# Attention stage of a hybrid block: scores first, and the weighting between the two maxima

## The chip, the cores and the metric

One core of one Trainium2 chip runs the whole program. The metric is the device time in microseconds (us); the kernel before has a median of 874.27 us over three runs (874.11 to 877.36).

## What is computed

The input is 16 sequences of 256 rows of 128 numbers. The block runs a long convolution (S4D), a mixture of 8 experts with the two best per row, an attention with 16 heads of 8 numbers, and the mixture again:

```python
x = x + _L0_attn_a_ref(_layernorm(x, axis=-1), ...)
x = x + _L0_ffn_ref(_layernorm(x, axis=-1), ...)
x = x + _L0_attn_b_ref(_layernorm(x, axis=-1), L0_attn_b_Wqkv, L0_attn_b_Wout)
x = x + _L0_ffn_ref(_layernorm(x, axis=-1), ...)
```

The change lies in the attention, of which this is the core:

```python
logits = jnp.einsum('bihd,bjhd->bhij', q, k) * scale
logits = logits + SLOPES[None, :, None, None] * rel[None, None, :, :]
logits = jnp.where(causal[None, None, :, :], logits, -jnp.inf)
attn = jax.nn.softmax(logits, axis=-1)
out = jnp.einsum('bhij,bjhd->bihd', attn, v).reshape(Bc, Tc, Dc)
return out @ Wout
```

## The kernel before

`attention_stage` (line 1730) handles one sequence (a batch, b) after another, 16 in all, and each in 4 quarters of 4 heads (G = 0 to 3); quarter x is 4b + G, so there are 64. The softmax needs the largest logit of each row before the exponential. It is found by a first set of score matmuls, rows of queries against keys, whose result VectorE reduces; the row maxima then travel through two transposes and a small DMA into two rows of the operand QPAD, so that the second set of score matmuls (keys against queries) yields logits with the maximum already subtracted.

Every engine runs a program written out by hand, in order, and meets the others at semaphores. On TensorE (`quarter_of`, line 2056) a quarter has these blocks:

- `maxima(y, 0)` and `maxima(y, 1)` (lines 1956 to 1973): the first set, four masking matmuls (L1953) and four score matmuls (L1970) on half-height (64 row) tiles of the array. Tile 0 gives 512 numbers per partition, tile 1 gives 1024. Both write banks 2 and 3, so each waits (`m_red`) until VectorE's reduction (L2226) of the other has read them. They run 4 and 5 quarters ahead.
- `scores(x)` (L1947, L1994, L1998): the second set, also on 64 row tiles, into banks 5 to 7. It waits (`exps`) until ScalarE has read the quarter before. In quarters 0 and 2 it also waits for the DMA of the row maxima (`mrow_in`, L1859).
- `weigh(x - 1)` (L2027, L2028): probabilities times values, f32, on tiles of 128 rows by 32 columns, into half of bank 4. It waits for the exponential of its quarter and, in every second quarter, until ScalarE's `take_out` (L2152) has emptied bank 4 (`ot_set`).
- transposes and projections on the whole array: G = 0 `turn_out` (L2045) and `project` (L1933), G = 1 `project_out` (L2053) and `values` (L1941), G = 2 and 3 `turn_maxima` (L1978) and `turn_back` (L2039). In a few batches G = 3 also has the gate or the ranks of the expert choice (`route.gate`, `route.rank`).

ScalarE's order in a quarter: in G = 1 `take_out` of the batch before, in G = 2 `values` and the normalised rows of an earlier batch (`batches.scalar`, L1134), in G = 3 `take_out` of this batch; then `expo` (L2148) on banks 5 to 7; then `out_high` (L2157) and `highs` (L2133) in G = 0 and `maxima_rows` (L2143) in G = 2 and 3. VectorE: the reduction of tile 0, one or two small operations, the reduction of tile 1, further small ones (`split`, L2218, in G = 1 behind the first reduction). SyncE's queue per batch: load of the spread queries and keys (L1849, L1852), their store (L1842, six DMAs, once `split` is done), the row maxima of both halves (L1859, two DMAs each), the transposes for the next stage (L1143). GpSimd takes each finished batch (row statistics of L2248): norm scalars (L1111 to L1121), rows (L1126, L1127), and for 16 of the tiles the sending to the expert lists (L1058, L1071).

Of the kernel before, what the change touches and what calls it, by code (L numbers as in the profile page):

```python
# [1729 lines left out]
def attention_stage(nc, t):  # L1730
# [13 lines left out]
    with ExitStack() as ctx:  # L1744
# [50 lines left out]
        def after(eng, s, n):  # L1795

            if n > 0:
                eng.wait_ge(s, n)
# [6 lines left out]
        def batch(c):  # L1805
            return 0 <= c < NB

        def quarter(x):
            return 0 <= x < LAST

        def gate_group(b):

            return (b - 7) // 4 if b >= 7 and (b - 7) % 4 == 0 and (b - 7) // 4 < ROUTED_IN_ATTENTION else None

        def rank_group(b):

            early = gate_group(b - 2)
            return early if early is not None and early < SENT_IN_ATTENTION else last_rank(b)
# [104 lines left out]
        def _(pe):  # L1923
# [20 lines left out]
            def mask_later(out, a, half, start):  # L1944

                first = HALF * (a + 1 - half)
                pe.matmul(out[:, :, HALF * half:HALF * half + HALF], LATER_ROWS[PAIR[a], first:first + P],  # L1947
                          LATER[PAIR[a], :, HALF * a:HALF * a + HALF], start=start, stop=False, skip_group_check=True)
# [7 lines left out]
            def maxima(y, tile):  # L1956

                c, G = divmod(y, HG)
                if G == 0 and tile == 1:
                    pe.wait_ge(qk_in[c % 3], 48 * (c // 3 + 1))  # L1960
                after(pe, m_red, 2 * y + 1 - tile)
                keys, queries = P * tile + P, slice(P * tile, P * tile + P)
                out = [ps[2 + a][:, 0:2 * keys].rearrange("p (s n) -> p s n", n=keys) for a in range(2)]
                for a in range(2):
                    mask_earlier(out[a][:, :, P * tile:P * tile + P], a, 0, True)
                for a in range(2):
                    mask_earlier(out[a][:, :, P * tile:P * tile + P], a, 1, False)
                for s in range(2):
                    for a in range(2):
                        ins = pe.matmul(out[a][:, s], QPAD[c % 3][PAIR[a], s, G, queries], KST[c % 3][PAIR[a], G, 0:keys],  # L1970
                                        start=False, stop=True, skip_group_check=True)
                        if s == 1:
                            ins.then_inc(m_mm, 1)

            def turn_maxima(c, h):
                pe.wait_ge(m16, 2 * c + h + 1)
                for tile in range(TPB):
                    ins = pe.transpose(ps[0].bitcast(F16)[0:16, P * tile:P * tile + P],  # L1978
                                       M16[:, h, tile].rearrange("p s a i -> p (s a i)"), ID16)
                ins.then_inc(mt_mm, 1)  # L1980

            def scores(x):

                c, G = divmod(x, HG)
                if G % 2 == 0:
                    pe.wait_ge(mrow_in[G // 2], 32 * (c + 1))
                if x == 0:
                    pe.wait_ge(middle.low, 4)
                after(pe, exps, x)
                early = [ps[5 + a].rearrange("p (h t n) -> p h t n", t=TPB, n=P)[:, :, 0] for a in range(2)]  # L1990
                late = [ps[7][:, SEQ * a:SEQ * a + SEQ].rearrange("p (h n) -> p h n", n=P) for a in range(2)]

                def early_scores(a):
                    return pe.matmul(ps[5 + a], KST[c % 3][PAIR[a], G, 0:P], QPAD[c % 3][PAIR[a], :, G, :], start=False,  # L1994
                                     stop=True, skip_group_check=True)

                def late_scores(a):
                    return pe.matmul(ps[7][:, SEQ * a:SEQ * a + SEQ], KST[c % 3][PAIR[a], G, P:2 * P],  # L1998
                                     QPAD[c % 3][PAIR[a], :, G, P:2 * P], start=False, stop=True, skip_group_check=True)
                mask_later(late[0], 0, 0, True)  # L2000
                mask_later(early[1], 1, 0, True)
                mask_later(late[0], 0, 1, False)
                mask_later(early[1], 1, 1, False)
                late_scores(0).then_inc(st_mm, 1)
                early_scores(1)
                mask_later(early[0], 0, 0, True)
                mask_later(early[0], 0, 1, False)
                pe.wait_ge(st_mm, 3 * x + 1)
                mask_later(late[1], 1, 0, True)
                mask_later(late[1], 1, 1, False)  # L2010
                early_scores(0).then_inc(st_mm, 1)
                late_scores(1).then_inc(st_mm, 1)

            def weigh(x):

                c, G = divmod(x, HG)
                pe.wait_ge(exps, x + 1)
                if G == 0:
                    pe.wait_ge(vset, c + 1)
                if G % 2 == 0:  # L2020
                    after(pe, ot_set, 2 * c + G // 2)
                half = ps[4][:, SEQ * (G % 2):SEQ * (G % 2) + SEQ]
                for g in range(GH):
                    out = half[32 * g:32 * g + 32, :]
                    early = PR[G % 2][:, g // 2, SEQ * (g % 2):SEQ * (g % 2) + SEQ]
                    late = PR[G % 2][:, 2, P * g:P * g + P]
                    pe.matmul(out, V32[c % 2][:, 0, 4 * G + g, :], early, start=True, stop=False)  # L2027
                    ins = pe.matmul(out[:, P:2 * P], V32[c % 2][:, 1, 4 * G + g, :], late, start=False, stop=True)  # L2028
                ins.then_inc(av_mm, 1)
# [12 lines left out]
            def turn_out(c):  # L2042
                pe.wait_ge(att, 2 * c + 2)
                for tile in range(TPB):
                    ins = pe.transpose(ps[1][:, P * tile:P * tile + P], ATT[:, tile, :], t.ID)  # L2045
                ins.then_inc(fa_mm, 1)
# [8 lines left out]

            def quarter_of(b, G):
                x = HG * b + G
                if quarter(x + 4):
                    maxima(x + 4, 0)
                if quarter(x):  # L2060
                    scores(x)
                if G == 3:
                    if gate_group(b) is not None:
                        for c in range(4 * gate_group(b), 4 * gate_group(b) + 4):
                            batches.landed(pe, c)
                        after(pe, mrow_set, min(2 * b + 3, 2 * NB))
                        route.gate(pe, gate_group(b), ps[0])
                    if rank_group(b) is not None:
                        after(pe, mrow_set, min(2 * b + 3, 2 * NB))
                        route.rank(pe, rank_group(b), ps[0])  # L2070
                if quarter(x + 5):
                    maxima(x + 5, 1)
                if G == 0:
                    if batch(b - 2):
                        turn_out(b - 2)
                    if batch(b + 3):
                        project(b + 3)
                if G == 1 and batch(b - 2):
                    project_out(b - 2)
                if G == 2:  # L2080
                    if batch(b + 1):
                        pe.wait_ge(vset, b + 2)
                        turn_maxima(b + 1, 0)
                    if batch(b - 1):
                        turn_back(b - 1, 0)
                if G == 3:
                    if batch(b + 1):
                        after(pe, mrow_set, 2 * b + 3)
                        if gate_group(b) is not None:
                            route.logits_taken(pe, gate_group(b))  # L2090
                        if rank_group(b) is not None:
                            route.ranks_taken(pe, rank_group(b))
                        turn_maxima(b + 1, 1)
                    if batch(b - 1):
                        turn_back(b - 1, 1)
                if b == -1 and G == 0:
                    middle.turn(pe, 2)
                    middle.turn(pe, 3)
                if b == 0:
                    middle.turn(pe, 4 + G)  # L2100
                if quarter(x - 1):
                    weigh(x - 1)
                if G == 1 and batch(b + 1):
                    values(b + 1)

# [370 lines left out]
```

## Time and profile before

| what | value |
|---|---|
| median of three runs | 874.27 us (874.11 to 877.36) |
| time of the profiled execution | 877.4 us, of which the span of the trace is 875.6 us |
| TensorE busy over the span | 618.8 us (71%) |
| VectorE busy | 622.3 us (71%) |
| ScalarE busy | 443.5 us (51%) |
| GpSimd busy | 458.8 us (52%) |
| first and last exponential of the attention | start at 415.3 and 628.2 us |

The span is the time between the first and the last instruction of one execution. Matmuls are pipelined, so the time of one in a row is its passage, not what the next one waits; the distance between the starts of two blocks is what a block costs. PE is TensorE's matmul side, PEld its weight loads, DVE VectorE, ACT ScalarE, POOL GpSimd, SPq the queue of SyncE.

### The profile page before, as it was taken

What the parts mean: (1) busy time and instruction counts of PE and PEld (TensorE: products, weight loads), DVE (VectorE), ACT (ScalarE), POOL (GpSimd) and SP (SyncE); (2) the same over time, 40 slices, a digit from 0 to 9 for tenths busy, and PEclk for the clock granted to TensorE, in tenths of its full rate; (3) what the DMA queues carried; (4) which work ended last, traced back from release to release, by engine and by line L of the source; (5) the groups of instructions that cost most, each with busy time, mean ns of one, the idle gap of its engine ahead of it and who ended that gap; (6) DMA issues with size and microseconds to landing.
All of it is one profiled execution on the core that took longest, in us unless ns stands there. A gap on an engine that the chain in (4) does not pass through costs nothing. (4 is left out here: it accounts for less than half of the span.)

```text
span 875.6 us, 21952 instructions
## 1 busy us (share of the span) xinstructions
PE 618.8 (71%) x7826; PEld 454.7 (52%) x7826; DVE 622.3 (71%) x1397; ACT 443.5 (51%) x873; POOL 458.8 (52%) x591
## 2 busy tenths in 40 slices
PE   0569975780089999125899999999714884999950
PEld 0354433560069999113556666655502563999940
DVE  6997887682078888387778888888513872888856
ACT  5634456760045556162767666666603332555534
POOL 1238758887557777410003223565765880677760
PEclk9968987995579999755899999999956996999985
DMA  9510002341044554332123233241110412444518
GB/s 287 144 38 1 0 8 70 71 90 50 32 83 90 94 94 89 132 116 70 57 64 90 67 88 87 80 119 52 42 34 28 83 34 48 85 100 96 100 28 283
DMA packets 131850, 70.51 MB, mean 81 GB/s; under 512 B 89535, under 2 KB 118725, under 8 KB 131746
## 3 DMA queue, kind: packets, MB, share of 16 engines
q1 hardware_dynamic: 121042, 50.46, 23.9%
q0 software_dynamic: 9088, 16.88, 6.8%
q10 hardware_dynamic: 1616, 1.77, 0.7%
q8 instruction: 67, 1.10, 0.5%
q14 instruction: 37, 0.30, 0.1%
HBM read 26.61 MB, written 30.50 MB: 65 GB/s over the span
## 5 line engine op out<-in xcount | busy, mean ns | idle before, releaser
L1500 ACT ACTIVATE ARENA<-banks,ARENA 128x256 f32<-128x256 f32 x312 | 122.3, 476 | 98.7 <-PE banks L1460 94.4
L2226 DVE TENSOR_REDUCE ARENA<-banks 128x4 f32<-128x1024 f32 (+1 forms) x128 | 122.8, 959 | 39.2 <-PE banks L1970 37.7
L1458 PE MATMUL banks<-ARENA,W1H 128*128 128x256 f16 x312 | 88.1, 282 | 62.3 <-DMA ARENA<-slots 61.5
L2148 ACT ACTIVATE ARENA<-banks 128x1536 f32<-128x1536 f32 x64 | 92.7, 1448 | 38.2 <-PE banks L1994 38.2
L1472 PE MATMUL banks<-W2L,ARENA 128*128 x624 | 110.0, 219 | 2.3 <-DVE ARENA L1513 2.3
L1474 PE MATMUL banks<-W2H,ARENA 128*128 x624 | 109.7, 219 | 0.0
L1473 PE MATMUL banks<-W2H,ARENA 128*128 x624 | 109.7, 219 | 0.0
L1448 POOL DMA_INDIRECT expert_out_g<-ARENA x78 | 77.8, 997 | 48.8 <-issue 26.2
L1448 POOL DMA_INDIRECT expert_out_f<-ARENA x78 | 81.4, 1043 | 33.1 <-issue 23.5
L1532 DVE TENSOR_TENSOR ARENA<-ARENA 128x1024 f16<-128x1024 f32 x78 | 95.6, 1225 | 2.7
L1058 POOL DMA_INDIRECT slots<-ARENA,PLACE x64 | 77.4, 1210 | 26.0 <-issue 17.5
L1459 PE MATMUL banks<-ARENA,W1H 128*128 128x256 f16 x312 | 88.0, 282 | 0.0
L1460 PE MATMUL banks<-ARENA,W1L 128*128 128x256 f16 x312 | 87.9, 282 | 0.0
L1071 POOL DMA_INDIRECT slots<-ARENA,PLACE x64 | 77.3, 1208 | 19.1 <-issue 14.6
L1530 DVE CAST ARENA<-ARENA 128x1024 f16<-128x1024 f32 x78 | 55.0, 706 | 35.0 <-ACT ARENA L1500 34.7
L1458 PEld LDWEIGHTS banks<-ARENA,W1H 128*128 x312 | 31.5, 101 | 67.6 <-issue 63.6
L1472 PEld LDWEIGHTS banks<-W2L,ARENA 128*128 128x128 f16 x624 | 61.0, 98 | 4.1 <-issue 2.9
L1473 PEld LDWEIGHTS banks<-W2H,ARENA 128*128 128x128 f16 x624 | 61.0, 98 | 1.6
L1474 PEld LDWEIGHTS banks<-W2H,ARENA 128*128 128x128 f16 x624 | 61.0, 98 | 0.0
L1953 PE MATMUL banks<-ARENA 64*128 64x128 bf16 x512 | 37.9, 228 | 29.3 <-DVE ARENA L2226 16.9
L488 PE MATMUL banks<-XN,ARENA 128*128 128x512 f32 x64 | 33.7, 688 | 34.2 <-ACT XN L395 29.8
L1518 DVE COPY ARENA<-B 128x4 f32 x78 | 17.8, 282 | 45.9 <-issue 45.9
(324 smaller groups left out, 1773.2 us busy)
## 6 DMA issues: line engine op xcount, KB each, us to landing
spread<-ARENA SPq DMA_DIRECT2D x96, 64.0 KB
ARENA<-expert_out_f SPq DMA_DIRECT2D x8, 512.0 KB, 7.6
ARENA<-spread SPq DMA_DIRECT2D x16, 256.0 KB, 3.0
ARENA<-spread SPq DMA_DIRECT2D x32, 128.0 KB, 2.8
ARENA<-expert_out_g SPq DMA_DIRECT2D x8, 512.0 KB, 7.3
XT<-in_w SPq DMA_DIRECT2D x10, 256.0 KB, 7.7
slots<-EMPTY SPq DMA_DIRECT2D x16, 129.0 KB, 4.3
ARENA<-in_w SPq DMA_DIRECT2D x8, 256.0 KB, 6.6
```

What stands on the lines that cost most here:

```text
L1058: nc.gpsimd.indirect_dma_start(xs, bass.IndirectOffsetOnAxis(ap=t.PLACE[:, 0, i:i + 1], axis=0), ROWI[:, i, :], None).then_inc(sent[i % GR ...
L1448: nc.gpsimd.indirect_dma_start(yo, bass.IndirectOffsetOnAxis(ap=target, axis=0), Y[i % 4][:, h], None, bounds_check=2 * NT * P - 1, oob_is ...
L1458: pe.matmul(out, t.W1H[:, e, ms], XST[i][:, 0], start=True, stop=False)
L1459: pe.matmul(out, t.W1H[:, e, ms], XST[i][:, 1], start=False, stop=False)
L1460: ins = pe.matmul(out, t.W1L[:, e, ms], XST[i][:, 0], start=False, stop=True)
L1472: pe.matmul(out, hh, t.W2L[:, e, m, :], start=(m == 0), stop=False)
L1473: pe.matmul(out, hh, t.W2H[:, e, m, :], start=False, stop=False)
L1474: ins = pe.matmul(out, hl, t.W2H[:, e, m, :], start=False, stop=(m == MT - 1))
L1500: ins = nc.scalar.activation(HF[i % 2][:, m], UP[i % 2][:, m], ACT.Gelu, bias=BIAS[i % 4][:, m:m + 1], scale=1.0 / WS)
L1532: dve.tensor_tensor(H16[i % 4][:, 1], HF[i % 2], H16[i % 4][:, 0], ALU.subtract).then_inc(split, 1)
L2148: nc.scalar.activation(PR[x % 2], t.psum_all[:, 5:8, :], ACT.Exp, scale=1.0 / LOGIT).then_inc(exps, 1)
L2226: dve.tensor_reduce(MX[:, G // 2, tile, :, :, G % 2].rearrange("p s a -> p a s"), src, AX.X, ALU.max).then_inc(m_red, 1)
```

## The change

Only TensorE's `quarter_of` is altered. `scores(x)` comes ahead of `maxima(x + 4, 0)`, and `weigh(x - 1)` moves from behind the transposes and projections to directly behind `maxima(x + 4, 0)`, ahead of the gate or ranks and of `maxima(x + 5, 1)`. No instruction is added or removed, no buffer and no semaphore changes, and the other engines' programs stay as they are.

```diff
             def quarter_of(b, G):
                 x = HG * b + G
+                if quarter(x):
+                    scores(x)
                 if quarter(x + 4):
                     maxima(x + 4, 0)
-                if quarter(x):
-                    scores(x)
+                if quarter(x - 1):
+                    weigh(x - 1)
                 if G == 3:
                     if gate_group(b) is not None:
...
                 if b == 0:
                     middle.turn(pe, 4 + G)
-                if quarter(x - 1):
-                    weigh(x - 1)
                 if G == 1 and batch(b + 1):
                     values(b + 1)
```

## Rows read from the trace of the kernel before

**Rows 1.** Page, granted TensorE clock in 40 slices of the span, tenths of full speed.

```profile
PEclk9968987995579999755899999999956996999985
```

**Rows 2.** Waits between 440 and 600 us: who waited for whom; total us, times, longest.

```profile
ACT ARENA L2148 <- PE banks L1994: 30.5, 38, 2.1
...
PEld banks L1953 <- DVE ARENA L2226: 17.9, 58, 0.4
```

**Rows 3.** Timeline, TensorE, batch 2, G = 0: start us, us, engine, line, count [idle before].

```profile
444.50 0.29 PE L1953 MATMUL banks<-ARENA 64*128 64x128 bf16 x4
...
444.74 0.28 PE L1947 MATMUL banks<-ARENA 64*128 64x128 bf16 x4
...
445.30 0.27 PE L1998 MATMUL banks<-ARENA 64*128 64x256 f16 x1
...
445.72 0.11 PEld L1953 LDWEIGHTS banks<-ARENA 64*128 64x128 bf16 x4 [0.38 <-DVE ARENA L2226]
...
446.15 0.44 PE L2045 MATMUL banks<-ID,ARENA 128*128 128x128 f32 x2
...
446.32 0.21 PEld L1933 LDWEIGHTS banks<-XT,QKWH 128*128 128x128 f16 x2
...
446.98 0.27 PE L1933 MATMUL banks<-XT,QKWL 128*128 128x256 f16 x1
...
447.18 0.66 PE L2027 MATMUL banks<-ARENA 128*32 128x256 f32 x8
...
447.99 0.28 PE L1953 MATMUL banks<-ARENA 64*128 64x128 bf16 x4
```

**Rows 4.** Timeline, VectorE, the two reductions of the same quarter.

```profile
444.97 0.69 DVE L2226 TENSOR_REDUCE ARENA<-banks 128x4 f32<-128x512 f32 x1 [0.24 <-PE banks L1970]
...
446.29 1.23 DVE L2226 TENSOR_REDUCE ARENA<-banks 128x4 f32<-128x1024 f32 x1 [0.63 <-PE banks L1970]
```

**Rows 5.** Timeline, ScalarE, batch 2, and the first exponential of batch 3.

```profile
445.64 1.45 ACT L2148 ACTIVATE ARENA<-banks 128x1536 f32<-128x1536 f32 x1 [1.64 <-PE banks L1994]
...
447.29 0.60 ACT L2133 ACTIVATE ARENA<-banks 128x512 f16<-128x512 f32 x1
448.15 0.60 ACT L2152 ACTIVATE ARENA<-banks 128x512 f32<-128x512 f32 x1 [0.27 <-PE banks L2028]
449.13 1.45 ACT L2148 ACTIVATE ARENA<-banks 128x1536 f32<-128x1536 f32 x1 [0.38 <-PE banks L1994]
...
459.07 1.45 ACT L2148 ACTIVATE ARENA<-banks 128x1536 f32<-128x1536 f32 x1 [1.64 <-PE banks L1994]
```

**Rows 6.** Timeline, TensorE, G = 1 of batch 2: values, then the next maxima.

```profile
450.88 0.11 PEld L1941 LDWEIGHTS banks<-VOWH,XT 128*128 128x128 f16 x2 [0.20 <-issue]
...
451.33 0.29 PE L1953 MATMUL banks<-ARENA 64*128 64x128 bf16 x4
```

**Rows 7.** Timeline, TensorE, batch 15: scores directly behind a weighting.

```profile
619.93 0.28 PE L1947 MATMUL banks<-ARENA 64*128 64x128 bf16 x4
...
620.50 0.27 PE L1998 MATMUL banks<-ARENA 64*128 64x256 f16 x1
```

**Rows 8.** SyncE's queue (stores, row maxima), and time to landing of line L1852.

```profile
449.82 4.32 SPq L1842 DMA_DIRECT2D spread<-ARENA  x6
454.20 4.34 SPq L1859 DMA_DIRECT2D ARENA<-ARENA  x4
...
495.08 3.74 SPq L1859 DMA_DIRECT2D ARENA<-ARENA  x4
...
DMA to landing us min/median/max: 2.5/2.8/4.6
```

**Rows 9.** Timeline, GpSimd, where it takes batches 11 and 12.

```profile
608.64 0.20 POOL L1111 TENSOR_TENSOR NRM<-RSTATS 128x2 f32<-128x2 f32 x1 [5.97 <-DVE RSTATS L2248]
...
621.01 0.20 POOL L1111 TENSOR_TENSOR NRM<-RSTATS 128x2 f32<-128x2 f32 x1
```

**Rows 10.** Timeline, ScalarE in batch 12, G = 2.

```profile
588.79 0.88 ACT L1134 ACTIVATE XN<-RES,NRM 128x128 f32<-128x128 f32 x2 [1.78 <-POOL NRM L1121]
```

## The prediction, written before the changed kernel was run

> **What bounds the kernel now.** I read the page first. It shows no engine that is full over the span (TensorE and VectorE 71% each), so a stage must be read by itself. Its row of clocks [rows 1] shows TensorE at 9 tenths or more in the slices of the attention from about 440 us on; so what follows is at the higher level of 2.4 GHz, and the first batch, which starts at a lower granted clock, is left out of the sum. Then the waits of the steady part [rows 2]: ScalarE's exponential waits for the scores, 30.5 us, but that engine is not full and pays nothing for it; TensorE waits for VectorE's reduction 58 times, up to 0.4 us, 17.9 us in all. That wait is what the new order goes at. Last the timeline of one quarter [rows 3]. TensorE goes from the first maxima (444.50) to scores (444.74), second maxima (445.72), transposes and projections (446.15), weighting (447.18) and the next first maxima (447.99): 3.49 us with one real stall, the 0.38 us ahead of the second maxima. Exponentials follow each other at 3.4 us on average: 459.07 less 445.64 is 13.43 us a batch [rows 5]. So TensorE's order sets the pace from 440 us on, with VectorE's reductions folded into it.
>
> **The fixed chain inside the quarter.** First maxima at 444.50, reduction at 444.97, 0.69 us long, second maxima at 445.72 [rows 3, 4]: 0.47 + 0.69 + 0.06 = 1.22 us that no order shortens. Before, scores lie in it; they end early, so TensorE stands. Afterwards the weighting lies in it.
>
> **Do the blocks fit?** Weighting to next block is 447.99 - 447.18 = 0.81 us, first maxima 0.24, and one more change of the array's tiles. What such a change costs: L2045 to L1933, both on the whole array, follow each other without a gap (weights at 446.32), while from 446.98 (L1933) to 447.18 (L2027, 32 columns) there are 0.20 us where a matmul of 256 columns streams for about 0.11 (I read that from six L1933 between 446.32 and 446.98). So a change costs about 0.1 us. 0.24 + 0.1 + 0.81 = 1.15 us, under the 1.22: the second maxima still start 1.22 us after the first, with 0.07 to spare.
>
> By the Trainium skill's page "TensorEngine Tiling (Array Packing)", Key Properties, changing the tiling mode drains TensorE. The trace agrees, by the 0.20 us above; the rule speaks against this order, which sets a weighting between two blocks of one mode that had been neighbours. Without a cost of such changes the same sum would leave 0.17 us to spare and gain nothing more, because the chain of 1.22 us holds either way.
>
> **The sum of a quarter.** Before: 1.22 + 0.43 (second maxima to transposes) + 1.03 + 0.81 (weighting) = 3.49. After: 1.22 + 0.43 + 1.03 + scores. Scores behind a tile change take 619.93 to 620.50, 0.57, plus 0.11 for the last one's columns [rows 7]: 0.68. So 3.36 us, 0.13 less. That is all that is left of the 0.38 us stall: the weighting (0.81) goes under the reduction's cover and the scores (0.68) come out of it. G = 0, 2 and 3 gain this each. In G = 1 `values` stands alone behind the weighting today, 450.88 to 451.33 [rows 6]; it then follows `project_out` in the same mode and a change (0.1) goes: 0.22 us.
>
> **The reduction of the second maxima.** It starts 0.57 us after them, takes 1.23 and releases at 0.06: 1.86 us from second maxima to first maxima. After the change that way holds 0.43 + the projections + 0.68: 2.14 in G = 0. The other three quarters share 13.43 - 3.49 = 9.94 us, 3.31 each, so their projections are on average 0.18 shorter, and the way is about 1.96. It just fits; if VectorE is late by 0.1 the stall comes back there.
>
> **What becomes late.** In G = 1 the weighting waits for `take_out`, which stands on ScalarE behind `highs`, and that waits for `project`, now the last block of G = 0. From the last L1933 (446.98) `highs` begins at 0.31, ends at 0.91 [rows 3, 5]; `take_out`, 0.60, ends at 1.51, less some 0.1 by which neighbours on ScalarE overlap; TensorE wants to weigh at 0.20 + 0.68 + 0.24 + 0.10 = 1.22. Late by 0.25 to 0.34, of which 0.07 hide under the reduction: I take 0.2; bounds 0 (if `highs` starts earlier than 0.31, where it stood behind another one) and 0.35. Before, weighting and first maxima (0.81 + 0.24) covered all this. Behind the waiting weighting stand the second maxima, so the loss is whole. The exponential of that quarter starts 0.2 late as well, but needs only to be done by the next scores, 3.3 us on, after 1.45: free. The batch gains 3 x 0.13 + 0.22 - 0.2 = 0.41 us.
>
> **How many batches count.** GpSimd takes batch 11 at 608.64 after 5.97 us of idle time, but batch 12 at 621.01 with none [rows 9]: from there on its own chain of norms and sends carries the stage to its end, and quarters saved later are worth nothing. Around batch 12 ScalarE waits 1.78 us for GpSimd inside the quarter [rows 10]; a faster TensorE only waits longer there. I count 12 of 16 batches (1 to 11, and 13): 12 x 0.41 = 4.9 us.
>
> **SyncE's queue.** The scores get ahead of everything else by the weighting, 0.8 us, and the batch is 0.4 shorter: the row maxima have 1.2 us less to arrive. The queue issues six stores from 449.82 to 454.14, then the row maxima at 454.20 [rows 8]; the scores that need them come 0.90 ahead of 459.07 [rows 3, 5], at 458.17. No view gives the landing of these transfers of 4 KB; the nearest row, 128 KB ones, has 2.5 to 4.6, median 2.8. With the second issue 0.6 after the first, a landing of 2.8 would leave 0.6 us of slack today; I take 1.7 for so little data, and 1.7 us of slack, 0.5 after the change. At 495.08 the same issue is 0.6 later than three batches of 13.43 after 454.20: there the slack goes and a batch pays about 1 us. Bounds: no batch pays, or every one (below). 4.9 - 1.0 = 3.9 us.
>
> The profiled execution took 877.4 us, 3.1 above the median of its runs; it would become 873.5, and the median 874.27 - 3.9 = 870.4 us.
>
> **Rivals.**
> - More is gained: `take_out` isn't late and no row maxima are, 13 batches x 0.61 = 7.9 us, 866.4 us. For it: the 0.31 us is measured behind another operation. Against: `take_out` itself is 0.60. Chance 0.18.
> - It is given back: VectorE's small operations between the reductions are late by the 0.1 that is left, or GpSimd's chain starts from the same place; 0 to 2 us remain, 873.5 us. For it: both margins, 1.15 under 1.22 and 1.86 under 1.96, are 0.1 us or less. Chance 0.27.
> - Slower, by one mechanism: the row maxima's DMA ends last. If it lands 2.8 us after its issue and the store queue is as late as at 495.08, the scores of G = 0 wait 0.6 + 0.6 = 1.2 us in each of 13 batches: 15.6 - 4.9 gives 885 us. With the first half alone it is 7.8 - 4.9, 877.2 us. It decides from a slack below 1.2 us today. Against: the exponential of G = 0 comes as regularly as the others (13.43). Chance of the full form 0.09, of the half 0.08.
> - The forecast: 0.38.
>
> **The numbers.** 0.5%, 4.4 us, is about what a measurement of this kernel tells from no change. Faster than 869.9: the first rival and a half of the forecast's spread of 868.5 to 872.5, 0.38. Slower than 878.6: 0.10. Within: 0.52. The range reaches from 866.2 to 877.0; outside lie the full DMA case and some of both edges.
>
> **What would show it.** In the trace after: the 0.38 us ahead of L1953 gone or under 0.15, L2027 between two L1953; exponentials 3.36 us apart in G = 0 and 13.0 a batch; an idle time of 0.2 to 0.3 us ahead of L2027 in G = 1, released by L2152; GpSimd's batch 11 taken 3 to 5 us earlier and batch 12 again without idle time. It is wrong if a wait of L1947 for L1859 shows in most batches, if second maxima start more than 1.3 us after the first, or if the batch stays at 13.4.

## The result and the profile after

The changed kernel has a median of 873.37 us over 11 runs (869.38 to 876.40), the kernel before 876.00 us over the 11 runs beside it (874.11 to 877.54). The ratio is 0.9964, 95% interval 0.9948 to 0.9979: by the ratio 3.2 us less (1.8 to 4.6), with the forecast at 3.9. The medians themselves are 2.6 us apart.

The 11 runs of the kernel before spread over 3.4 us and those of the changed one over 7.0, and in the traces the first exponential of the attention starts anywhere from 413.4 to 415.7 us, though nothing ahead of it was changed. What follows the attention varies too: from the start of the next stage to the end of the span it is 210.5 us in the trace before and 211.7 in the trace after. So the traces are compared by the stage alone: from the first exponential to GpSimd's first norm of the next stage (L1205). The first fence is the timeline of the kernel before, the second that of the changed one; start, duration, engine, line:

```profile
415.32 1.42 ACT L2148 ACTIVATE ARENA<-banks 128x1536 f32<-128x1536 f32 x1
...
665.09 0.71 POOL L1205 TENSOR_TENSOR NRM<-NRM,MHALF 128x2 f32<-128x2 f32 x1 [11.91 <-DVE NRM L86]
```

```profile
415.35 1.42 ACT L2148 ACTIVATE ARENA<-banks 128x1536 f32<-128x1536 f32 x1
...
663.01 0.71 POOL L1205 TENSOR_TENSOR NRM<-NRM,MHALF 128x2 f32<-128x2 f32 x1 [11.91 <-DVE NRM L86]
```

The stage went from 249.8 to 247.7 us, 2.1 less in this execution. Another execution of the same changed kernel (e1 below) has 247.4.

The waits of the steady part, 440 to 600 us, of the changed kernel (total us, times, longest), against [rows 2]:

```profile
ACT ARENA L2148 <- PE banks L1994: 21.0, 26, 2.5
...
PEld banks L1953 <- DVE ARENA L2226: 7.7, 27, 0.4
...
PE banks L2027 <- ACT ARENA L2152: 2.7, 10, 0.3
ACT XN L1134 <- POOL NRM L1121: 1.9, 1, 1.9
PEld banks L1947 <- DMA ARENA<-ARENA: 1.9, 2, 1.7
```

The idle time put down to VectorE's reduction fell from 17.9 to 7.7 us. Those 7.7 are 27 gaps of about 0.28 us, of which 0.20 is the change of tiles described below. Two waits are new: the weighting for `take_out`, and the scores for the row maxima's DMA.

The same batch as in [rows 3 to 5], G = 0 and the start of G = 1, from the timeline of the changed kernel:

```profile
444.73 0.29 PE L1947 MATMUL banks<-ARENA 64*128 64x128 bf16 x4
...
445.33 0.17 PEld L1953 LDWEIGHTS banks<-ARENA 64*128 64x128 bf16 x4
445.41 0.27 PE L1953 MATMUL banks<-ARENA 64*128 64x128 bf16 x4
...
445.73 0.66 PE L2027 MATMUL banks<-ARENA 128*32 128x256 f32 x8
445.87 0.69 DVE L2226 TENSOR_REDUCE ARENA<-banks 128x4 f32<-128x512 f32 x1
...
446.61 0.11 PEld L1953 LDWEIGHTS banks<-ARENA 64*128 64x128 bf16 x4 [0.28 <-DVE ARENA L2226]
446.62 0.28 PE L1953 MATMUL banks<-ARENA 64*128 64x128 bf16 x4
...
447.05 0.44 PE L2045 MATMUL banks<-ID,ARENA 128*128 128x128 f32 x2
...
448.08 0.29 PE L1947 MATMUL banks<-ARENA 64*128 64x128 bf16 x4
...
448.18 0.60 ACT L2133 ACTIVATE ARENA<-banks 128x512 f16<-128x512 f32 x1 [0.27 <-PE banks L1933]
...
448.67 0.59 ACT L2152 ACTIVATE ARENA<-banks 128x512 f32<-128x512 f32 x1
...
449.15 1.46 ACT L2148 ACTIVATE ARENA<-banks 128x1536 f32<-128x1536 f32 x1
...
449.41 0.66 PE L2027 MATMUL banks<-ARENA 128*32 128x256 f32 x8 [0.27 <-ACT ARENA L2152]
...
450.95 0.15 PEld L1941 LDWEIGHTS banks<-VOWH,XT 128*128 128x128 f16 x2
...
451.44 0.29 PE L1947 MATMUL banks<-ARENA 64*128 64x128 bf16 x4
```

Scores to scores is 3.35 us in G = 0 (444.73 to 448.08), where it took 3.49 in the kernel before. The weighting runs beside the reduction (445.73 and 445.87); the second maxima follow the weighting after 0.28 us, of which 0.20 is the gap that stands at such a change of tiles without any wait (the `[0.20 <-issue]` of [rows 6]) and 0.08 still waits for VectorE. In G = 1 the weighting waits for `take_out`, which starts behind `highs` at 448.67; this quarter takes 3.36 us (448.08 to 451.44) and gains nothing.

From one G = 0 exponential to the next G = 0 exponential an undisturbed batch takes 13.04 us, where it took 13.43. The whole stage by batches, from the starts of ScalarE's exponentials:

| first exponential of batch | before | after | difference |
|---|---|---|---|
| 2 | 445.64 | 445.64 | 0 |
| 7 | 512.77 | 510.86 | -1.9 |
| 10 | 553.57 | 550.75 | -2.8 |
| 11 | 567.00 | 565.29 | -1.7 |
| 12 | 580.84 | 578.85 | -2.0 |
| 13 | 594.91 | 593.65 | -1.3 |
| GpSimd takes batch 11 | 608.64 | 607.82 | -0.8 |
| next stage | 665.09 | 663.01 | -2.1 |

Two places give back a part of what was gained. At the end of batch 10 the scores wait for the row maxima. Changed kernel, SyncE's queue, TensorE and ScalarE:

```profile
560.64 3.25 SPq L1859 DMA_DIRECT2D ARENA<-ARENA  x4
...
564.37 0.29 PE L1947 MATMUL banks<-ARENA 64*128 64x128 bf16 x4 [1.42 <-DMA ARENA<-ARENA]
...
565.29 1.45 ACT L2148 ACTIVATE ARENA<-banks 128x1536 f32<-128x1536 f32 x1 [2.51 <-PE banks L1994]
```

And in batch 12 ScalarE waits for GpSimd, 1.92 us where it was 1.78 [rows 10], and the next quarter's scores wait for ScalarE. That wait costs TensorE more than before, because the scores now head the quarter and nothing goes ahead of them; in the old order the first maxima had been issued and their reduction ran meanwhile. The scores in the kernel before, then in the changed one:

```profile
591.06 0.28 PE L1947 MATMUL banks<-ARENA 64*128 64x128 bf16 x4 [0.89 <-ACT ARENA L2148]
```

```profile
589.52 0.29 PE L1947 MATMUL banks<-ARENA 64*128 64x128 bf16 x4 [1.48 <-ACT ARENA L2148]
```

GpSimd itself, on batches 11 and 12, against [rows 9]:

```profile
607.82 0.20 POOL L1111 TENSOR_TENSOR NRM<-RSTATS 128x2 f32<-128x2 f32 x1 [6.45 <-DVE RSTATS L2248]
...
612.94 0.40 POOL L1126 CAST ARENA<-XN 128x256 f16<-128x256 f32 x1
...
619.26 0.21 POOL L1111 TENSOR_TENSOR NRM<-RSTATS 128x2 f32<-128x2 f32 x1
```

It takes batch 11 only 0.8 us earlier. But ScalarE begins the normalised rows of this batch (L1134) at 612.01 where it was 613.74, 1.7 us earlier, so GpSimd finds them ready: L1126 has no idle time ahead of it, where it had 0.97 us in the kernel before. It takes batch 12 at 619.26 against 621.01, 1.75 us earlier.

### The profile page after: what moved, and what is told of

Read it like the earlier page. It is cut to its first block and busy times, and to the rows that moved or that the text cites. A ratio compares the mean times of both kernels' runs of the same rounds, so it can differ in the third digit from the quotient of the medians.

```text
span 874.7 us, 21952 instructions
## 1 busy us (share of the span) xinstructions
PE 620.5 (71%) x7826; PEld 459.0 (52%) x7826; DVE 618.3 (71%) x1397; ACT 444.2 (51%) x873; POOL 462.3 (53%) x591
## 5 line engine op out<-in xcount | busy, mean ns | idle before, releaser
L1448 POOL DMA_INDIRECT expert_out_g<-ARENA x78 | 81.6, 1047 | 46.0 <-issue 23.5
L1111 POOL TENSOR_TENSOR NRM<-RSTATS 128x2 f32<-128x2 f32 x15 | 3.0, 198 | 93.0 <-DVE RSTATS L2248 92.9
```

Of the source, the lines that this page charges most:

```text
L1448: nc.gpsimd.indirect_dma_start(yo, bass.IndirectOffsetOnAxis(ap=target, axis=0), Y[i % 4][:, h], None, bounds_check=2 * NT * P - 1, oob_is ...
```

## The experiments

Stage lengths in the table are from one trace each, times from all runs. e1 to e4 were measured together, so were e5 to e8, and e9 to e11.

| run | us a batch | stage, us | ratio to before, 95% interval |
|---|---|---|---|
| before | 13.43 | 249.8 | 1 |
| e1 changed kernel again | 13.05 | 247.4 | 0.9970 (0.9954 to 0.9986) |
| e2 take_out early | 12.79 | 245.1 | 0.9953 (0.9936 to 0.9970) |
| e3 store split | 13.04 | 246.4 | 0.9960 (0.9945 to 0.9975) |
| e4 both | 12.79 | 243.6 | 0.9932 (0.9916 to 0.9948) |
| e5 scores first alone | 16.12 | 286.5 | 1.0431 (1.0401 to 1.0462) |
| e6 weighing moved alone | 14.66 | 268.9 | 1.0215 (1.0185 to 1.0244) |
| e7 half reduction, before | 12.35 | 239.6 | 0.9863 (0.9834 to 0.9892) |
| e8 half reduction, after | 12.71 | 244.1 | 0.9925 (0.9894 to 0.9957) |
| e9 both, again | 12.79 | 243.6 | 0.9926 (0.9913 to 0.9940) |
| e10 sends spread | 12.79 | 243.9 | 0.9927 (0.9913 to 0.9941) |
| e11 late weighing | 13.05 | 246.3 | 0.9948 (0.9929 to 0.9966) |

**e5 and e6, the two halves of the change.** Each moves one block of the kernel before:

```diff
 e5                                      e6
+                if quarter(x):              if quarter(x): scores(x)
+                    scores(x)           +   if quarter(x - 1): weigh(x - 1)
                 if quarter(x + 4):          ...
                     maxima(x + 4, 0)    -   if quarter(x - 1): weigh(x - 1)
-                if quarter(x):
-                    scores(x)
```

> Of the kernel before only scores and first maxima change places; the weighting stays at the end of the quarter. Theory (first maxima, reduction and second maxima are a fixed chain of 1.22 us, and something must lie in it): nothing lies in it, so a quarter is 1.22 + 0.43 + 1.03 + 0.81 + 0.68 = 4.17 us in G = 0, 0.68 more than before; about 16 us a batch, over 12 batches 33 us slower. Rival (the gain comes from starting the exponential earlier): faster than before or the same.

> First maxima, scores, weighting, second maxima, projections: only the weighting is moved. Theory: first to second maxima 0.24 + 0.57 + 0.15 + 0.81 = 1.77 us, TensorE-bound; then the second reduction (1.86 us from second to first maxima) has only 0.43 + 1.03 = 1.46 us of cover in G = 0 and 1.2 in the others, so it becomes the stall: 3.63 us a quarter, 14.5 a batch, 13 us slower than before. Rival (more cover for the first reduction is all that counts): as the changed kernel or faster.

Both halves alone are slower, beyond their intervals. TensorE in e5, start of a quarter of G = 0:

```profile
479.23 0.28 PE L1953 MATMUL banks<-ARENA 64*128 64x128 bf16 x4
...
480.44 0.29 PE L1953 MATMUL banks<-ARENA 64*128 64x128 bf16 x4 [0.82 <-DVE ARENA L2226]
```

First to second maxima is 1.21 us with nothing in it: the chain of 1.22 is there whatever lies beside it. The batch is 16.12 us, 2.69 more than before, the scores' 0.68 four times; the stage is 36.7 us longer, where 33 were expected. In e6 the weight loads show the stall on the other side:

```profile
478.45 0.11 PEld L1953 LDWEIGHTS banks<-ARENA 64*128 64x128 bf16 x4 [0.20 <-issue]
...
479.06 0.21 PEld L1933 LDWEIGHTS banks<-XT,QKWH 128*128 128x128 f16 x2
...
480.31 0.12 PEld L1953 LDWEIGHTS banks<-ARENA 64*128 64x128 bf16 x4 [0.61 <-DVE ARENA L2226]
```

Second to first maxima is 1.86 us (478.45 to 480.31), as worked out ahead of the run; all four quarters are 3.66 us. The gain of the change is in the pair: one of the two blocks of 0.7 to 0.8 us under each reduction, the larger one under the first.

**e7 and e8, the reduction itself halved**, in the kernel before and in the changed one:

```diff
                 src = t.psum_all[:, 2:4, 0:2 * keys].rearrange("p a (s n) -> p a s n", n=keys)
+                if tile == 0:
+                    src = src[:, :, :, 0:keys // 2]
```

> The kernel before with the first reduction reading 64 of 128 keys (the maxima of tile 0 are so computed from half of the keys). Theory (the reduction is in TensorE's chain there): it falls from 0.69 to 0.42 us and the stall ahead of the second maxima by as much, 0.27 x 4 = 1.1 us a batch, 12.35 a batch. Rival (tile changes and issue make the stall): no more than 0.1 a quarter.

> The same halved reduction in the changed kernel (maxima of tile 0 from half of the keys). Theory (the weighting with its tile changes nearly fills the chain): only the 0.08 us that the second maxima still wait in G = 0 and 2 and 0.14 in G = 3 can go, nothing in G = 1, 0.3 us a batch, 12.75. Rival (the chain is still bound by the reduction with room to spare): 1.1 us a batch as in the kernel before.

The reduction takes 0.43 us in place of 0.69. The old order gains 1.08 us a batch and the new one 0.33, as the chain says: what the new order brings is cover. With a shorter reduction the old order is the faster one, by 0.36 us a batch. Nearly all of that lies in G = 1, whose weighting waits for `take_out` in the new order only. Weight loads of TensorE, from one quarter's first block to the next one's, e7 and then e8:

```profile
469.36 0.11 PEld L1953 LDWEIGHTS banks<-ARENA 64*128 64x128 bf16 x4 [0.20 <-issue]
...
472.43 0.11 PEld L1953 LDWEIGHTS banks<-ARENA 64*128 64x128 bf16 x4
```

```profile
470.11 0.11 PEld L1947 LDWEIGHTS banks<-ARENA 64*128 64x128 bf16 x4 [0.21 <-issue]
...
471.42 0.21 PEld L2027 LDWEIGHTS banks<-ARENA 128*32 128x32 f32 x8 [0.41 <-issue]
...
473.47 0.12 PEld L1947 LDWEIGHTS banks<-ARENA 64*128 64x128 bf16 x4
```

G = 1 takes 3.07 us in e7 and 3.36 in e8, 0.29 apart; the other three quarters together differ by 0.07, though each has one more change of tiles in the new order. So these runs do not isolate what a change of tiles costs. In e8 the wait for the row maxima is there again, once for 1.5 us. It is in e7 too, with TensorE's old order and a batch of 12.35 us: 1.2 us in three places.

**e1 to e4, the two new waits.** e1 is the changed kernel. e2 moves one line of ScalarE:

```diff
-                if G == 1 and batch(b - 1):
-                    take_out(b - 1, 1)
                 if G == 3 and batch(b):
...
                     expo(x)
                 if G == 0:
+                    if batch(b - 1):
+                        take_out(b - 1, 1)
                     if batch(b - 2):
                         out_high(b - 2)
```

e3 splits SyncE's stores (`store_qk` now takes the range of stores to issue; its own lines are left out here), and e4 has both:

```diff
-                    store_qk(b + 3)
+                    store_qk(b + 3, 0, 4)
                 if batch(b + 1):
                     spread_m(b + 1, 0)
+                if batch(b + 3):
+                    store_qk(b + 3, 4, 6)
+                if batch(b + 1):
                     spread_m(b + 1, 1)
```

> The changed kernel, unaltered, as the reference of this group. The same for all theories: 0.9964 of the kernel before, 13.04 us a batch in the undisturbed batches, the weighting of G = 1 late by 0.25 us behind take_out, one wait of about 1.4 us for the row maxima in batch 10 or 11 if that wait comes from the order of SyncE's queue and of GpSimd's sends; somewhere else or nowhere if it is chance.

> ScalarE's take_out of the second half of the batch before stands in G = 0 directly behind the exponential, ahead of out_high and highs. Theory (the weighting of G = 1 waits for take_out): that gap of 0.45 us ahead of L2027 falls to 0.15, of the 0.30 some 0.08 come back as a wait for the reduction, so 0.2 us a batch less, 12.84 a batch, and over 12 batches 2.4 us less than the changed kernel. Rival (row maxima end last): the slack of their DMA, 0.5 us in the changed kernel, shrinks to 0.3, more batches wait for it and the time stays.

> SyncE issues four of the six stores of queries and keys ahead of the first row maxima and two behind them. Theory (the stores in front make the row maxima late): the row maxima are issued 0.5 us earlier in every batch, the waits of the scores for them in batches 9 to 11 go, 1 us less than the changed kernel; batches stay at 13.04. Rival (the landing itself is slow there, by GpSimd's sends on the same DMA engines): the wait in batch 11 stays, no difference.

> Both orders together. Theory: 12.84 us a batch, no wait for row maxima, 2.4 + 1 = 3.4 us less than the changed kernel, some 0.75% less than the kernel before. Rival: GpSimd's chain takes most of it, since batches 8 to 10 are already near its pace; then under 1.5 us less.

In e1 the wait for the row maxima is at the end of batch 10 again, 1.1 us, and also at the end of batch 7, 0.8 us; e11, which has the same order, has next to none. So the order opens the place for it, and chance decides how much is paid there.

In e2 the batch is 12.79 us, 0.25 less where 0.2 was expected: what the late weighting had cost in G = 1, with no other wait in its place there. The rival is right in part: the scores wait for the row maxima four times, in batch 6 too. Even so e2 keeps 2.3 us of stage over e1. Timeline of e2, G = 1: the weighting directly behind the first maxima, and only the reduction's 0.08 left ahead of the second:

```profile
447.95 0.27 PE L1970 MATMUL banks<-ARENA 64*128 64x128 f16 x4
...
448.15 0.66 PE L2027 MATMUL banks<-ARENA 128*32 128x256 f32 x8
...
449.04 0.11 PEld L1953 LDWEIGHTS banks<-ARENA 64*128 64x128 bf16 x4 [0.28 <-DVE ARENA L2226]
```

The wait for the row maxima is in e1 (2.1 us in three places) and in e2, in the weight loads' column of waits:

```profile
PEld banks L1947 <- DMA ARENA<-ARENA: 2.4, 4, 1.6
```

In e3 and e4 no such row exists. SyncE's queue in batch 10 shows why, first of the changed kernel and then of e3, where the same lines stand three numbers further down:

```profile
555.82 4.78 SPq L1842 DMA_DIRECT2D spread<-ARENA  x6
560.64 3.25 SPq L1859 DMA_DIRECT2D ARENA<-ARENA  x4
```

```profile
554.61 2.52 SPq L1845 DMA_DIRECT2D spread<-ARENA  x4
558.50 1.22 SPq L1862 DMA_DIRECT2D ARENA<-ARENA  x2
559.77 1.21 SPq L1845 DMA_DIRECT2D spread<-ARENA  x2
```

The two executions began the batch at different times, so the issue is counted from the batch's first exponential (550.75 and 549.67): 9.89 us in the changed kernel, 8.83 in e3. In e3 it is 8.83 in every batch; in the changed kernel it wanders from 8.9 to 9.9 over batches 2 to 10, so the split gains 0.1 us in one batch and 1.1 in another.

Of the executions traced with the old queue order behind the changed TensorE order, four (the changed kernel, e1, e2, e8) have a longest wait of 1.1 to 1.7 us for this DMA and one (e11) has 0.6 us in all; of the four with the split (e3, e4, e9, e10) none has any. So the rival, that the wait stays whatever the order, falls. It had a point: where the scores waited at the end of batch 10, they began 3.1 to 3.7 us after the first issue of the row maxima, against 2.3 to 2.5 where they waited for them in other batches. With the split they begin 3.3 us after it and don't wait. Whether the shorter way in front of the DMA also makes its landing quicker, these runs don't tell. e3's gain in time over e1 is within their intervals; in the traces it is 1.0 us of stage. e4 is the fastest version here: 0.9932, in the traces 6.2 us less than before, 3.8 less than e1. That is more than the 3.4 expected. e9 repeats it at 0.9926.

**e10, GpSimd's sends over four batches**, on top of e4:

```diff
                     if c == 4 * g + 8:
                         route.dispatch_first(pool, g, range(GRP // 2, GRP))
-                        route.dispatch_second(pool, g, (0,))
                     if c == 4 * g + 9:
+                        route.dispatch_second(pool, g, (0,))
+                    if c == 4 * g + 10:
                         route.dispatch_second(pool, g, (1,))
```

> The kernel with both orders (take_out early, store split) again, as the reference of this group: 0.993 of the kernel before, 12.79 us in the undisturbed batches, 2.2 us of waiting for GpSimd in batch 12.

> Both orders, and GpSimd's 16 sends of a group go 4, 4, 4, 4 over four batches in place of 4, 8, 4 over three. Theory (GpSimd is late for batch 9 because of the 8 sends in one batch, ScalarE's exponential in batch 12 waits for it, and everything up to GpSimd's batch 11 counts): the wait of 2.2 us in batch 12 goes, batch 11 is taken 2 us earlier, the next stage starts 2 us earlier. Rival (GpSimd's chain is bound as a whole from batch 7 on): the wait only moves and the next stage starts at the same time.

The wait in batch 12 went, and GpSimd took batch 11 at 600.79 with its first exponential at 414.31, against 602.88 and 414.52 in e9: 1.9 us earlier. The next stage didn't move (243.9 us after the first exponential, 243.6 in e9). GpSimd's last batch and the next stage in e10:

```profile
634.29 0.21 POOL L1111 TENSOR_TENSOR NRM<-RSTATS 128x2 f32<-128x2 f32 x1
...
644.01 0.96 POOL L1071 DMA_INDIRECT slots<-ARENA,PLACE  x1 [0.30 <-issue]
658.25 0.72 POOL L1205 TENSOR_TENSOR NRM<-NRM,MHALF 128x2 f32<-128x2 f32 x1 [13.28 <-DVE NRM L86]
```

For the second group the same spreading moved four sends behind the last batch's norms: GpSimd takes the last batch 6.5 us earlier after the first exponential than in e9, but finishes its last instruction only 1.1 us earlier. The idle time ahead of the next stage grew from 11.91 to 13.28 us; what fills it isn't shown. So the rival's outcome came, the next stage at the same time, though the wait went and did not move. Whether spreading the first group alone would keep the 1.9 us was not tried.

**e11, more work for TensorE at the end of the stage:**

```diff
-                for g in range(GH):
+                for g in [g for _ in range(4 if x >= LAST - 2 else 1) for g in range(GH)]:
```

> The changed kernel with the weighting of the last two quarters issued four times over (the same numbers again), some 2.4 us more of TensorE in each, 4.9 us in all. Theory (from GpSimd's batch 11 on its chain alone sets the end of the stage): the next stage starts as long after the first exponential as in the changed kernel, 247.5 us, within 0.5. Rival (TensorE still sets the end): 252 us.

The first and the last of the four weightings in one of the two quarters:

```profile
623.92 0.66 PE L2027 MATMUL banks<-ARENA 128*32 128x256 f32 x8
...
625.89 0.69 PE L2027 MATMUL banks<-ARENA 128*32 128x256 f32 x8
```

The three repeats took 1.97 us in each quarter, 3.9 us in all and not the 4.9 expected. The next stage starts 246.3 us after the first exponential, 1.1 to 1.4 less than in the two traces of the changed kernel, whose waits of over 1 us for the row maxima this execution lacks; e3, which has none of them either, stands at 246.4. So 3.9 us more of TensorE in the last two quarters cost nothing: TensorE doesn't end the stage. That GpSimd's chain does is read from its rows, where it takes each batch from batch 12 on without idle time; no run shows it by itself.

## Why the prediction was right

- *The fixed chain of 1.22 us* was right, and e5 shows it bare.
- *The fit of the weighting*, 1.15 in 1.22, was right: 0.08 us of waiting is left in place of 0.07. e8 measures what is left of the stall by halving the reduction, 0.33 us a batch.
- *The sum of a quarter*: 3.36 forecast for G = 0, 3.35 measured from scores to scores. G = 2 went from 3.25 to 3.12 and G = 3 from 3.35 to 3.21 (block starts), 0.13 and 0.14 where 0.13 was forecast. The exponentials, though, were forecast 3.36 us apart in G = 0 and are 3.51 (445.64 to 449.15): `take_out`, late behind `highs`, delays ScalarE's next exponential, which gives the time back in the quarters behind it.
- *G = 1*: forecast 0.22 - 0.20 = 0.02 us gained, measured 0.02 lost. `take_out` was late by 0.3, as in the upper bound, and e2 gives its price as 0.25 us a batch where I took 0.20. That makes up the difference between 0.41 and the measured 0.38 us a batch.
- *The second reduction* gave no stall worth naming: 1.86 us, which e6 shows bare, fit beside the other blocks.
- *The row maxima*: one collision of about 1 us was forecast, at the place near 495 us where the queue had been late. The mechanism was right and its place wrong: it came at the end of batch 10, for 1.4 us (1.7 in the weight loads). The other batches show no wait of note, as a landing of 1.7 us has it: where the scores do wait in other batches, they begin 2.3 us after the first issue (in the changed kernel at 536.58, the issue being at 534.25), so 1.7 after the second. The median of 2.8 of the larger transfers would have stalled nearly every one.
- *How many batches count*: I counted batches 1 to 11 and 13 at the full 0.41 us. Batches 2 to 6 gave 0.38 each, but batch 1 nothing, and 7 to 9, which hold the gate, the ranks and VectorE's steps of the expert choice, 0.25 to 0.34: 2.8 us at the start of batch 10. Batch 11 gave 0.28. Batch 12, put at 0, took 0.73 us more than before (14.80 against 14.07): "a faster TensorE only waits longer there" left out that the wait now stands at the head of the quarter and holds up the first maxima as well. Batch 13 took 0.45 less. At the start of batch 14 1.7 us were gained (608.08 to 606.37).
- *GpSimd's batch 11* was to be taken 3 to 5 us earlier; this sign failed, it is taken 0.8 us earlier. What I had not counted: VectorE's statistics (L2248), which start GpSimd's batch, come behind the first reduction, and that now comes later beside the scores; of the 1.7 us only 0.8 get there. This cost nothing in the end, because GpSimd had waited 0.97 us for its normalised rows and these come 1.7 us earlier; so 2.1 us stand at the end. Batch 12 was again taken without idle time, as forecast, and e11 shows that TensorE's last quarters don't set the end.

The forecast of 3.9 us lies inside the measured interval, 1.8 to 4.6 us, but above what the stage itself gained, 2.1 us in the first trace and 2.4 in e1. The mis-sized terms nearly all erred to one side: the pace by 0.03 x 12 = 0.4, the collision by 0.5 (batch 10 lost 1.5 us against its neighbours' pace), batch 12 by 0.7, batches 1, 7 to 9 and 11 by 0.7, batch 13 by 0.1 the other way. That leaves 1.7 us at batch 14; GpSimd's side adds 0.4. So the mechanism was right and the count of batches too generous, and that the 3.2 us by all runs come nearer to 3.9 than the stage does is luck: nothing here shows where the further 1 us would come from. The median was forecast at 870.4 and is 873.37; of these 3.0 us, 1.7 are the kernel before, 876.00 over 11 runs against 874.27 over three.

## What to carry to other kernels

Where two engines hand one buffer back and forth, write down each handover as a fixed time, and then ask which block of the waiting engine lies under it; a block moved under one handover comes out of another, and only the pair gives a gain (e5 and e6 cost 4.3% and 2.2%, together they save 0.4%). A block that is drawn ahead takes the slack of its other inputs with it: move their producers too, as e4 does, which took the gain of the stage from 2.4 us (e1) to 6.2. And find the first point from which another engine ends the stage: what is saved behind it doesn't count.

## What was not expected of the hardware

The undisturbed batches of one order repeat to 0.01 us from one execution to another, while the start of the stage moves by 2.3 us, what follows the stage took 207.8 to 211.7 us, and whole runs of the changed kernel spread over 7 us. So one trace, cut to its stage, told changes of 0.25 us a batch, 3 us in 870, that runs alone hardly separate (e1 and e2 overlap in their intervals). The small DMA of the row maxima is the exception: its wait comes and goes between executions of one order (1.7 us in one, 1.1 at most in the next, as the weight loads see it), and from its first issue to the scores that wait for it there are 2.3 to 2.5 us in most batches and 3.1 to 3.7 at the end of batch 10. GpSimd was sending then, but so it was in e11, where the scores began 2.7 us after the issue without a wait; the cause is open.
